# Next image's projections over the eight units of an attention loop, and units regrouped over neighbouring key heads

## The reference

```python
x = rmsnorm(tokens, norm_w)
q = x @ Wq                       # 16 query heads of 64
k, v = split(x @ Wkv)            # 8 key heads of 64, 8 value heads of 64
q, k = l2norm(q) * gq, l2norm(k) * gk
sim = q[h, g] @ k[h].T           # query heads 2h and 2h+1 use key head h
sim = tanh(sim / 50) * 50 / 8, causal mask, softmax
out = sum over g of attn @ v[h]  # 8 heads of 64
h = layernorm(h + out @ Wout)
```

## Time and profile before

| | |
|---|---|
| median of three runs | 1977.88 us |
| the profiled execution | 1977.19 us |
| its span, first to last instruction | 1975.5 us |
| mean granted TensorE clock | 0.967 |
| TensorE (PE) busy | 1827.4 us, 93% |
| VectorE (DVE) busy | 1122.4 us, 57% |
| ScalarE (ACT) busy | 870.6 us, 44% |
| GpSimd (POOL) busy | 399.7 us, 20% |

### The profile page before, as it was taken

The page is one execution under the profiler, slowest core; times in us unless marked ns, Lnnn a source line. Parts: engine busy times, 40 slices in busy tenths (PEclk is TensorE's granted clock), DMA queues, the critical chain, the costliest instruction groups (busy, mean ns, idle before and its releaser), DMA issues. The chain is left out here.

```text
span 1975.5 us, 31720 instructions
## 1 busy us (share of the span) xinstructions
PE 1827.4 (93%) x11768; PEld 1578.6 (80%) x11768; DVE 1122.4 (57%) x2084; ACT 870.6 (44%) x1073; POOL 399.7 (20%) x502
## 2 busy tenths in 40 slices
PE   5899999999969989999998998699999999999997
PEld 5788998988958877877887887587878787787876
DVE  8788888887866766675775674414142331414141
ACT  4654455556426764674775575122122222212221
POOL 2000000000111211121121112233332433333342
PEclk9999999999979999999999998799999999999999
DMA  5322222214011002000200100510000000000000
GB/s 170 109 78 86 87 79 108 94 54 142 23 37 61 23 16 81 23 16 18 86 24 8 66 23 16 236 44 22 0 23 1 22 23 1 22 0 22 1 11 12
DMA packets 17308, 97.10 MB, mean 49 GB/s; under 512 B 2937, under 2 KB 3065, under 8 KB 11650
## 3 DMA queue, kind: packets, MB, share of 16 engines
q1 hardware_dynamic: 17154, 94.96, 13.6%
HBM read 82.33 MB, written 24.15 MB: 54 GB/s over the span
## 5 line engine op out<-in xcount | busy, mean ns | idle before, releaser
L556 PE MATMUL conv<-w_hi,x_hi 128*128 128x368 f16 (+5 forms) x1320 | 355.1, 279 | 7.7 <-issue 5.7
L556 PE MATMUL conv<-w_lo,x_hi 128*128 128x368 f16 (+5 forms) x1320 | 356.0, 279 | 0.0
L556 PE MATMUL conv<-w_hi,x_lo 128*128 128x368 f16 (+5 forms) x1320 | 354.6, 279 | 0.0
L1322 ACT ACTIVATE raw_c<-ring,sh 128x512 f32<-128x512 f32 x128 | 88.1, 688 | 370.2 <-PE ring L1419 370.2
L1110 PE MATMUL mixed<-v,probs 128*128 128x65 f32 x1536 | 201.3, 282 | 22.6 <-DVE parts L990 19.3
L1419 PE MATMUL ring<-ha_hi,wh 128*128 128x512 f32 x512 | 207.8, 406 | 13.0 <-POOL ha_lo L1284 13.0
L1110 PEld LDWEIGHTS mixed<-v,probs 128*128 128x128 f32 x1536 | 185.6, 195 | 37.8 <-issue 22.8
L1284 POOL TENSOR_TENSOR ha_lo<-raw_c,ha_hi 128x512 fp32r<-128x512 f32 x128 | 164.9, 1288 | 210.1 <-DVE ha_hi L1334 210.1
L556 PEld LDWEIGHTS conv<-w_hi,x_hi 128*128 128x128 f16 x1320 | 192.8, 146 | 16.7 <-issue 8.4
L1419 PE MATMUL ring<-ha_lo,wh 128*128 128x512 f32 x512 | 205.4, 401 | 0.0
L1419 PE MATMUL ring<-hb_hi,wh 128*128 128x512 f32 x512 | 202.2, 395 | 0.0
(11 more groups left out here) (148 smaller groups left out, 3472.9 us busy)
## 6 DMA issues: line engine op xcount, KB each, us to landing
xt<-x_columns_in SPq DMA_DIRECT2D x12, 1163.0 KB, 5.6
xp<-x_patches_in SPq DMA_DIRECT2D x12, 1152.0 KB, 5.1
hidden_words<-hidden_weights_in SPq DMA_DIRECT2D x8, 1408.0 KB, 9.0
words<-hidden_words SPq DMA_DIRECT2D x32, 352.0 KB, 3.1
wh<-hidden_words SPq DMA_DIRECT2D x2, 4096.0 KB, 22.0
tokens<-planes SPq DMA_DIRECT2D x4, 1024.0 KB, 4.3
lines<-tokens SPq DMA_DIRECT2D x4, 1024.0 KB, 5.5
h<-tokens SPq DMA_DIRECT2D x4, 1024.0 KB, 6.8
```

The source lines that it names most:

```text
L556: ins = pe.matmul(out, xs[:, c, RI - 1 - i:RI - 1 - i + NR, :, x].rearrange("p r g -> p (r g)"), w, start=(t == 0), stop=(t == len(terms) ...
L1322: act.activation(raw[:, u % 4], bank, ACT.Gelu, scale=scale[:, m:m + 1]).then_inc(s_gelu, 1)
```

## The change

Each unit now holds one map of each of two neighbouring key heads: unit hd takes, of the key heads 2p and 2p + 1 with p = hd // 2, one query head each. The host puts the query weights and scales in that order (`paired`). The rows of a key block after the transpose are then two different key heads, as the projection leaves them, and the doubled copy `keys` goes. Steps 11 and 15 go too. The one copy out of a key bank is written to both units of the pair. In the mix, the even unit writes its scaled maps straight to `o` and the odd unit adds its own to them. `SLOTS` is rewritten. A mask that nothing read is gone.

```diff
 SLOTS = (
-    [("make", 0), ("make", 1), ("make", 2)],
-    [("sum", 0), ("root", 0), ("make", 4)],
-    [("make", 5), ("make", 6), ("scale", 0)],
-    [("sum", 1), ("root", 1), ("make", 3), ("make", 8)],
-    [("make", 9), ("make", 10)],
-    [("make", 11), ("make", 7), ("scale", 1)],
-    [("make", 12)],
-    [("make", 13), ("make", 14), ("make", 15)],
+    [("make", 0), ("make", 1)],
+    [("make", 2)],
+    [("make", 4), ("sum", 0), ("root", 0)],
+    [("make", 5), ("scale", 0)],
+    [("make", 6), ("make", 8)],
+    [("sum", 1), ("root", 1), ("make", 3), ("make", 9), ("make", 10)],
+    [("make", 7), ("scale", 1)],
+    [("make", 12), ("make", 13), ("make", 14)],
 )
...
-    order += [("make", 0, j) for j in (3, 7, 8, 9, 10, 11)] + [("scale", 0, 1)]
-    return order + [("make", 0, j) for j in (12, 13, 14, 15)]
+    order += [("make", 0, j) for j in (3, 7, 8, 9, 10)] + [("scale", 0, 1)]
+    return order + [("make", 0, j) for j in (12, 13, 14)]
...
-                        by = rn[:, tb].rearrange("p (h d) -> p h d", d=1)
-                        dve.tensor_tensor(heads[:, 0:QH], heads[:, 0:QH], by[:, 0:QH].to_broadcast([P, QH, DH]), ALU.mult)
-                        for m in range(2):
-                            ins = dve.tensor_tensor(keys[:, tb, :, m], heads[:, QH:],
-                                                    by[:, QH:].to_broadcast([P, HEADS, DH]), ALU.mult)
-                        ins.then_inc(s_qn, 1)
+                        by = rn[:, tb].rearrange("p (h d) -> p h d", d=1).to_broadcast([P, QH + HEADS, DH])
+                        dve.tensor_tensor(heads, heads, by, ALU.mult).then_inc(s_qn, 1)
...
-                        by = gamma[:, 4 * r:4 * r + 4].rearrange("p (h t) -> p h t", t=1).to_broadcast([P, 4, P])
-                        dve.tensor_tensor(kt[:, img % 2, 4 * r:4 * r + 4, P * tb:P * tb + P], bank, by,
-                                          ALU.mult).then_inc(s_emptied["keys"], 1)
+                        for m in range(2):
+                            by = gamma[:, m::2].rearrange("p (h t) -> p h t", t=1).to_broadcast([P, EB, P])
+                            ins = dve.tensor_tensor(kt[:, img % 2, m::2, P * tb:P * tb + P], bank, by, ALU.mult)
+                        ins.then_inc(s_emptied["keys"], 1)
...
-                        dve.tensor_tensor(parts[:], got[:, :, :, 0:DH], rl[:].to_broadcast([P, 2, 2, DH]),
+                        pair = o[:, img % 2, :, 2 * (hd // 2):2 * (hd // 2) + 2]
+                        dve.tensor_tensor(parts[:] if hd % 2 else pair, got[:, :, :, 0:DH], rl[:].to_broadcast([P, 2, 2, DH]),
                                           ALU.mult).then_inc(s_mixread, 1)
-                        dve.wait_ge(s_mixread, g * NH + n + 2)
-                        dve.tensor_tensor(o[:, img % 2, :, hd], parts[:, :, 0], parts[:, :, 1],
-                                          ALU.add).then_inc(s_o, 1)
+                        if hd % 2:
+                            dve.wait_ge(s_mixread, g * NH + n + 2)
+                            dve.tensor_tensor(pair, pair, parts[:], ALU.add).then_inc(s_o, 1)
...
-                                    ins = pe.matmul(out, probs[:, n % 4, m, at:at + P], v[:, img % 2, jb, hd],
+                                    ins = pe.matmul(out, probs[:, n % 4, m, at:at + P], v[:, img % 2, jb, 2 * (hd // 2) + m],
```

## The result

The changed kernel is slower. Over ten runs of each, its median is 2002.1 us against 1985.07 of the kernel before, which now drew a little slower than in the three runs shown; the ratio is 1.009, 95% interval 1.0065 to 1.0115. That is 18 us by the ratio and 17 by the medians. The profiled execution took 2001.74 us, 24.6 more than the 1977.19 of before, which lies near the fast end of that kernel's runs (1976.26 to 1994.9). The forecast was +5 and its range ended at 1996, so the measured median lies outside it.

The account below looks back on a forecast made before the run. TensorE, busy 613.8 of the attention stage's 649 us, was taken as the bound, its waits lost time. Terms 7.2 + 2.8 - 2.2 - 3.0 - 1.6 + 0 = +3.2, plus 2 for clock: +5 on 1977.2, 1983 us; range 1963 to 1996.

Parts of the forecast that it names:

- The transposes and scales: Eight transposes fewer in each of 15 loop images, 14.2 us; with group ends and shorter scales in the first image, 17 us.
- The waits: Sign to look for: TensorE's waits for `parts` in the attention stage rise from 22.7 us to about 40.
- for the words: Sign at 778 us, a group start: VectorE waits over 3 us for the words that `bits` needs.
- `scale` held step 12: Plain image: `scale` in unit 6, step 12 opening unit 7 with no unit between, a wait of 0.3 us.
- the group start: Mix 2 still waits for the word load: +1.4 us in groups two and three, -1.1 in the first and last.
- the image of `rms_sum`: Three groups: `rms_sum` waits for a later `sum`, `rms_scale` falls in a crowded unit; net +2.4 us each, +7.2.
- five places with longer waits: Longer waits can cost clock, about 1.7 us lost each; one of five places was given that price, +2 us.
- Plain images: Five images without extra group work: each gains 0.95 us from transposes and pays 0.9 in added waits, so zero.
- The bound of 4.4 for sum and root: VectorE's `sum` and `root` together: 4.2 us taken, upper bound 4.4, which would add 6 us over 15 images.
- The second, clock and port adding up: Rival: all five long waits bring half rate (8.5 us) and the port price holds (6): 1990 to 1996 us, chance 0.25.
- Group ends: Three group ends: waits total 2.8 us, up from 0.84, 0.79 and 0.83; less the transposes, -1.0 each, -3.0.
- The start of the stage: First image, made with nothing beside it: shorter scales and fewer transposes against one more key copy, -1.6 us.

Follow-up runs that it names:

- c1: Regrouped heads with the old slots, plus five unused VectorE instructions of 0.9 us in each group's second image; ratio 1.0016 to the kernel before.
- a2: The changed kernel with `rms_sum` one unit later, behind the `sum` it waits for; ratio 1.0019 to the kernel before, 14 us under the changed kernel.
- w1: The changed kernel with a group's first words loaded ahead of the stores of the group before; ratio 1.0039 to the kernel before.
- h1: The changed kernel with the slots of before, so regrouped heads without the new order; median 1959.39 us, ratio 0.9883 to the kernel before.
- c2: Regrouped heads with the old slots, plus three unused VectorE instructions in each group's second image; ratio 0.9899 to the kernel before.

## Why the prediction was wrong

It had the waits and nearly every place of them. Two terms were too small, the clock above all and the plain images, and together they took the result out of the range.

- **The transposes and scales, -17 us.** Somewhat high: eight transposes an image gave 0.8 us and not 0.95, 12 us in 15 images and not 14.2. Heads only measured -23, and there the waits before a mix shrank too, from 22.7 to 15.1 us.
- **The waits, from 22.7 to about 40 us.** Right in sum: 39, counting scores, key copies and `scale`, and 34.0 before a mix alone. ScalarE idled 4.4 us in three waits before `rms_sum`, VectorE 2.6 and 2.2 us for the words, where over 3 were forecast. `scale` held step 12 for 0.2 us once, where 0.3 an image were forecast. The working of the group start names four projections between mix 2 and mix 5; there are three, and its 12.9 us are the sum for three. In the image of `rms_sum`, 4.75 and 3.2 make 7.95 and not 8.05, which changes nothing.
- **"Of the five places with longer waits I give one that price: +2."** This term failed. Behind the waits of the three third images and the two group starts the clock fell in each case: about 28 us more at half rate in all, up to 14 us where 2 were given. The third images came out 12.2 us over their forecast and the first images 5.8. Over all twelve traces, 33 of the 34 waits of TensorE of more than 2.3 us between the first and the last score had the clock at half rate no later than 2.3 us after their end; the prediction had one case of half rate to go by, behind a wait of 1.52 us. c1 shows by itself that a wait of 3.36 us doubles. a2 and w1 fit: by the profiled images, taking away 7.1 and about 5 us of waits gave back 12.6 and 9.7.
- **Plain images, 0.** This term failed too, by 3.2 us in five images. Waits went from 0.18 to 1.3 us where the forecast went from 0.2 to 1.1. The transposes gave 0.15 less than taken, and the projection steps, split over more units, cost 0.3 more, which the prediction put at nothing. The bound of 4.4 for sum and root was too low in unit 2, where they took 4.77; in unit 5 they took 4.14. This goes with their place beside the masks, and so with the order: with order alone the two take 4.79 and 4.14, with heads alone 4.05 and 4.29, before 4.05 and 4.43.

  The Trainium skill, "SBUF — State Buffer", section "Who interferes with whom", says that a VectorE instruction with two SBUF inputs contends with a GpSimd one that reads SBUF. The trace agrees in kind: three of the four slow instructions have two such inputs and took 0.33 to 0.36 us beside a mask instead of 0.18. The fourth and slowest, at 819.70, has one. No run here changes the inputs alone.
- **The rivals.** The second, clock and port adding up, came nearest. It was given 0.25 and its own sum ended at 1996, because it priced each place at one half-rate stretch of 1.7 us, 8.5 in all, where the third images lost about 3.4 to 5 us each and a group start up to 3.4.
- **Group ends, -3.0.** Measured -1.9; the waits (1.57 and 1.16 us against 1.4 and 1.3) are right.
- **The other terms.** The start of the stage gave -0.9 for -1.6. The first score starts between 588.5 and 592.1 us in the twelve traces, so that difference says nothing. The last image's -1.6 was not forecast and is not explained.

What remains open is why the same wait of 2.1 us at a group start brought 17 us at half rate in one run (h1, 41.6 us for the image) and 3.4 in another (c2, 2.14 us, 35.6 us).

## What to carry to other kernels

Spreading TensorE's work evenly is no aim in itself where VectorE reads out a single buffer in order: place the lumps of the engine that frees the buffer, and count for each the TensorE time up to the wait. When a step is moved by a unit, list every semaphore that other lists of the schedule hold against it, here `rms_sum` on `sum`, `sum` on the squares, `bits` on a load. On a TensorE that is nearly full, count a wait of 1.5 us as its length and perhaps as much again, and one of 3 us as 6. Count work by what stands next to it as well: in this kernel a projection alone in its unit cost up to 0.2 us more than one with another behind it.

## What the runs showed of the hardware

A wait of 3.36 us in an otherwise dense stretch of matmuls was followed by 6.7 us at half rate in three cases (granted clock 0.72 over 12 us) and by 10.3 in a fourth (0.57). One of 1.55 us left the mix behind it at full speed (1.52 us for twelve matmuls), but in two of four cases the clock fell some 2 us later, for 3.4 us (0.83 over 10 us). Half rate can outlast its cause: behind a wait of 2.06 us TensorE ran for 17 us at a granted clock of 0.52 with no idle time in them. VectorE's 0.18 us instructions took 0.33 to 0.43 us beside a mask in the plain image shown above.
